# Moving the first units of the last MLP into attention steps 21 to 31, with their gating and modulation on ACT

## What is computed

```python
g1, b1, g2, b2, a1, a2 = jnp.split(cond, 6, axis=-1)          # per sequence, 128 numbers each
h = _layernorm(x) * g1[:, None, :] + b1[:, None, :]
q, k, v = ...                                                 # 16 heads of 8
attn = softmax(q k^T / sqrt(8));  o = attn v
o = o @ W_o.T + b_o
x = res1 + o * a1[:, None, :]                                 # gate the projection, add the residual
res2 = x
h = _layernorm(x) * g2[:, None, :] + b2[:, None, :]           # normalize, modulate
h = _gelu_tanh(h @ W_f1.T + b_f1) @ W_f2.T + b_f2
x = res2 + h * a2[:, None, :]
```

## Time and profile before

| | us |
|---|---|
| runs | 315.18, 310.84, 314.17 (median 314.17) |
| the profiled execution, its own time | 311.09 |
| its span | 309.2 |
| mean granted TensorE clock | 0.989 |
| PE busy | 277.3 (90%) |
| DVE busy | 241.7 (78%) |
| ACT busy | 188.9 (61%) |
| POOL busy | 175.6 (57%) |

### The profile page before, as it was taken

One profiled execution on the slowest core, in us unless ns is written; L12 is line 12 of the kernel. 1 busy time (PEld: TensorE's weight loads), 2 busy tenths in 40 slices (PEclk: granted clock), 3 DMA queues, 4 the chain that ended last, 5 costly groups with the idle time before them and its releaser, 6 DMA issues.

```text
span 309.2 us, 8237 instructions
## 1 busy us (share of the span) xinstructions
PE 277.3 (90%) x2900; PEld 154.6 (50%) x2900; DVE 241.7 (78%) x643; ACT 188.9 (61%) x355; POOL 175.6 (57%) x357
## 2 busy tenths in 40 slices
PE   2889999899889588799999999989868999999995
PEld 2444454454444345456656565656444445544444
DVE  5569999698899977688988888898955776776443
ACT  4457888788778547687778777776536222333330
POOL 8031765995996559677878696953345444223400
PEclk9999999999999989999999999999979999999999
DMA  7950000430340003425353444530000011011112
GB/s 240 329 117 2 2 0 4 112 102 2 94 119 2 0 7 85 123 71 155 88 152 102 128 121 106 149 77 8 4 4 4 0 34 34 2 34 35 35 36 68
DMA packets 26233, 21.58 MB, mean 70 GB/s; under 512 B 4400, under 2 KB 25552, under 8 KB 25936
## 3 DMA queue, kind: packets, MB, share of 16 engines
q1 hardware_dynamic: 25760, 20.37, 24.7%
q10 hardware_dynamic: 432, 0.67, 0.7%
HBM read 4.26 MB, written 2.10 MB: 21 GB/s over the span
## 4 chain that ended last, share of the span: by engine, by line
PE 55%; POOL 18%; DVE 14%; issue 9%; ACT 2%; DMA 1%; DVEq 0%; POOLq 0%; ACTq 0%
PE psum L280 47%; DVE mx L927 5%; POOL xn_tile L1121 2%; POOL q_rest L1066 2%; POOL q_part L1068 2%; DVE hid L874 2%; POOL q_part L1072 1%; POOL k_rest L1076 1%; PE psum L474 1%; PE psum L555 1%; DVE o_turn L934 1%; POOL rstd L1118 1%; PE psum L466 1%; PE psum L646 1%; PE psum L526 1%
## 5 line engine op out<-in xcount | busy, mean ns | idle before, releaser
L927 DVE TENSOR_REDUCE mx<-psum 128x8 f32<-128x1024 f32 x64 | 75.4, 1192 | 12.2 <-PE psum L280 11.8
L767 ACT ACTIVATE probs<-psum 128x1024 f32<-128x1024 f32 x64 | 65.5, 1023 | 11.8 <-PE psum L280 10.6
L280 PE MATMUL psum<-w_early,h0T 128*128 128x512 f32 x128 | 68.7, 622 | 0.0
L803 ACT ACTIVATE g_act<-psum,w_late 128x512 f32<-128x512 f32 x32 | 22.0, 688 | 44.7 <-PE psum L280 44.7
L280 PE MATMUL psum<-probs,v_pad 128*32 128x128 f32 x1024 | 41.7, 281 | 2.3 <-DVE o_turn L934 2.0
L280 PE MATMUL psum<-h2T,w_late 128*128 128x512 f32 x64 | 31.4, 607 | 0.0
L874 DVE SCALAR_TENSOR_TENSOR hid<-psum,rstd,gate 128x512 f32<-128x512 f32 x32 | 23.8, 743 | 8.2 <-PE psum L280 3.7
L280 PEld LDWEIGHTS psum<-probs,v_pad 128*32 128x32 f32 x1024 | 24.6, 109 | 10.4 <-ACT probs L767 3.8
L733 ACT ACTIVATE gate<-psum,rstd 128x512 f32<-128x512 f32 x32 | 22.0, 687 | 11.4 <-PE psum L280 6.8
L280 PE MATMUL psum<-g_act,w_late 128*128 128x512 f32 (+1 forms) x72 | 28.8, 545 | 0.0
L280 PE MATMUL psum<-k_st,q_st 64*128 64x128 bf16 x512 | 25.5, 220 | 1.9 <-DVE mx L927 1.9
(11 more groups left out here) (129 smaller groups left out, 551.5 us busy)
## 6 DMA issues: line engine op xcount, KB each, us to landing
q_st<-q_part SPq DMA_DIRECT2D x48, 128.0 KB
k_st<-k_part SPq DMA_DIRECT2D x48, 128.0 KB, 2.4
x_tok<-x SPq DMA_DIRECT2D x8, 256.0 KB, 7.4
out<-out_t SPq DMA_DIRECT2D x7, 256.0 KB, 2.3
w_late<-late SPq DMA_DIRECT2D x1, 1159.5 KB, 9.0
w_early<-early ACTq DMA_DIRECT2D x2, 256.0 KB, 5.3
k_st<-k_st SPq DMA_DIRECT2D x4, 128.0 KB, 5.0
q_st<-q_st SPq DMA_DIRECT2D x4, 128.0 KB
```

Source lines behind the costliest of these rows:

```text
L280: return nc.tensor.matmul(o, w, m, start=start, stop=stop, skip_group_check=shares)
L767: nc.scalar.activation(probs[:, n % 3, :, :, :].rearrange("p f j q -> p (f j q)"), psum[:, pair[0]:pair[1] + 1, :].rearrange("p a b -> p ( ...
L803: nc.scalar.activation(g_act[:, f, :], bank(2 + f % 2), ACT.Gelu_apprx_tanh, bias=wl("b_f1")[:, f:f + 1]).then_inc(c_gelu[f], 1)
L927: v.tensor_reduce(mx[:, c % 2, :, r, :], psum[:, pair[0]:pair[1] + 1, :].rearrange("p f (j k) -> p f j k", j=4), X_AXIS, ALU.max, negate=T ...
```

## The change

Nine units of the front stand in attention steps now, one in a step: proj 0 in step 21, res 0 in 23, proj 1 in 24, norm 0 in 25, res 1 in 27, proj 2 in 28, norm 1 in 29, res 2 in 30 and proj 3 in 31. Three of them (norm 1, res 2, proj 3) stood in `mlp(2)` and `mlp(3)` before. They all use bank 7 and take their turn in `SHARED_FILLS`; score fills keep all three pairs to the end. ACT gates the projections of groups 0 to 3, as scale times product plus a ready bias `b_gated` (one new DVE instruction in stage A), and modulates groups 0 and 1; the groups after these stay with DVE. `h2T` has two buffers. POOL's `layer_norm(0)` stands in step 24, `layer_norm(1)` in 28 and `layer_norm(2)` in 32.

```diff
--- before.py
+++ after.py
...
-FRONT = {27: ("proj", 0), 28: ("res", 0), 29: ("proj", 1), 30: ("norm", 0)}
-FRONT_END = {30: ("res", 1), 31: ("proj", 2)}
-FRONT_BANK = {("proj", 0): 5, ("res", 0): 6, ("proj", 1): 5, ("norm", 0): 6, ("res", 1): 5, ("proj", 2): 7}
-TWO_PAIRS = 27
+FRONT = {21: ("proj", 0), 23: ("res", 0), 24: ("proj", 1), 25: ("norm", 0), 27: ("res", 1), 28: ("proj", 2),
+         29: ("norm", 1), 30: ("res", 2), 31: ("proj", 3)}
...
-        if step >= TWO_PAIRS:
-            owner.append(0 if kind == "exp" else 1)
-        else:
-            owner.append(n % 2 if n < 2 * LEAD else n % 3)
+        owner.append(n % 2 if n < 2 * LEAD else n % 3)
...
+        if b in FRONT:
+            shared.append(FRONT[b])
...
-SHARED = {f: n for n, f in enumerate(SHARED_FILLS)}
+SHARED = {f: n for n, f in enumerate(f for f in SHARED_FILLS if f[0] != "res")}
...
-        h2T = sb("h2T", [D, GT])
+        h2T = sb("h2T", [D, 2, GT])
...
-                pe.wait_ge(shared_set, SHARED[fill] + 1)
+                if fill[0] == "res":
+                    pe.wait_ge(c_x2, fill[1] + 1)
+                else:
+                    pe.wait_ge(shared_set, SHARED[fill] + 1)
...
-                if g:
-                    pe.wait_ge(c_proj, g)
-                mm(bank(n), wl("wo"), tile_cols(feat, GRP * g, GRP)).then_inc(c_proj_mm, 1)
+                if g > 4:
+                    pe.wait_ge(c_proj, g - 4)
+                return mm(bank(n), wl("wo"), tile_cols(feat, GRP * g, GRP))
...
-                pe.wait_ge(c_proj, g + 1)
+                pe.wait_ge(shared_set, SHARED["proj", g] + 1) if g < 4 else pe.wait_ge(c_proj, g - 3)
...
-                n = FRONT_BANK[kind, g]
-                if (kind, g) == ("proj", 0):
-                    was, c, r = THIRD_PAIR_LAST
-                    pe.wait_ge(b_max if was == "max" else b_exp, 2 * c + r + 1)
-                if (kind, g) == ("norm", 0):
-                    pe.wait_ge(c_x2, 1)
-                if n == MISC_BANK:
-                    taken_out(SHARED_FILLS[-1])
+                shared_free(kind, g)
...
-                    output_projection(g, n)
+                    output_projection(g, MISC_BANK).then_inc(shared_mm, 1)
...
-                    residual(g, n)
+                    residual(g, MISC_BANK)
...
-                    normalized_features(g, n)
+                    normalized_features(g, MISC_BANK).then_inc(shared_mm, 1)
...
-                if b in FRONT_END:
-                    front(*FRONT_END[b])
...
-                if 2 < i < NG:
-                    output_projection(i, 7)
+                if 3 < i < NG:
+                    if i == 4:
+                        taken_out(SHARED_FILLS[-1])
+                    output_projection(i, 7).then_inc(c_proj_mm, 1)
...
+            def gate_projection(g):
+                act.wait_ge(shared_mm, SHARED["proj", g] + 1)
+                if g == 0:
+                    act.wait_ge(b_gated_set, 1)
+                if g:
+                    act.wait_ge(c_res_mm, g)
+                for s in range(GRP):
+                    b = GRP * g + s
+                    last = nc.scalar.activation(projT[:, s, :], bank(MISC_BANK)[:, s * P:(s + 1) * P], ACT.Identity,
+                                                bias=b_gated[:, b:b + 1], scale=mods[:, 4, b:b + 1])
+                last.then_inc(shared_set, 1)
+
+            def modulate(g):
+                act.wait_ge(shared_mm, SHARED["norm", g] + 1)
+                for s in range(GRP):
+                    b = GRP * g + s
+                    last = nc.scalar.activation(h2T[:, g % 2, s * P:(s + 1) * P], bank(MISC_BANK)[:, s * P:(s + 1) * P], ACT.Identity,
+                                                bias=mods[:, 3, b:b + 1], scale=mods[:, 2, b:b + 1])
+                last.then_inc(shared_set, 1)
+
...
+                kind, group = FRONT.get(b, (None, None))
+                if kind == "proj":
+                    gate_projection(group)
+                if kind == "norm":
+                    modulate(group)
...
+                    dve.wait_ge(bias_set, 2)
+                    v.tensor_tensor(b_gated[:, :], mods[:, 4, :], b_ov[:, :].to_broadcast([P, B]), ALU.mult).then_inc(b_gated_set, 1)
...
-                if b == 27:
-                    gate_projection(0, FRONT_BANK["proj", 0])
-                if b == 28:
-                    add_residual(0, FRONT_BANK["res", 0])
+                kind, group = FRONT.get(b, (None, None))
+                if kind == "res":
+                    add_residual(group, MISC_BANK)
...
-                if b == 31:
-                    statistics(1)
-                if b == 32:
-                    gate_projection(2, FRONT_BANK["proj", 2])
...
-                if b == 28:
-                    statistics(0)
-                if b == 29:
-                    gate_projection(1, FRONT_BANK["proj", 1])
-                if b == 30:
-                    modulate(0, FRONT_BANK["norm", 0])
-                    add_residual(1, FRONT_BANK["res", 1])
+                if kind == "res":
+                    statistics(group)
...
-                if b == 29:
-                    layer_norm(0)
-                if b == 32:
-                    layer_norm(1)
+                if b < B and FRONT.get(b - 1, (None, 0))[0] == "res" and FRONT[b - 1][1] < 2:
+                    layer_norm(FRONT[b - 1][1])
+                if b == B:
+                    layer_norm(2)
...
-            for g in range(2, NG):
+            for g in range(3, NG):
```

50 lines of the change are left out of this document (26 added, 24 removed).

## The result

The changed kernel takes 314.36 us (median of 22 runs, 311.6 to 318.0). The kernel before, run beside it, took 311.43 (22 runs, 309.12 to 315.52). The ratio is **1.0071 [1.0043, 1.0099]**: slower by a little, within the 2% that count as the same.

A forecast was written before the change was run, and what follows sets the result against it. PE, DVE or a chain through ACT was taken to bound each attention step, PE's order the last stage. 311.09 + 4.3 (steps) - 1.95 (last stage) + 0.2 (`b_gated`) = 313.6; 2.5 added to the middle, 312.6, gave 315.1 us, range 310.0 to 319.5.

The forecast's parts named there:

- step 30: Attention step with res 2, without maxima: from 6.8 us to 2.6, with no POOL wait and no low clock left.
- norm steps: Steps 25 and 29: PE waits for `xn` from POOL about 1.1 and 1.5 us; steps of 5.1 and 5.2 us.
- last stage: MLP stage: `mlp(2)` falls from 5.15 to 4.06 us, `mlp(3)` loses its output projection of 0.86; together -1.95 us.
- gating chain: Steps 21, 24, 28: late weighing, score block, projection, ACT's four gating instructions, exponential, next weighing; 4.53 us, taken as 4.5.
- Rival 3: ACT's gating and modulating instructions don't overlap, 0.46 us start to start instead of 0.35: +2.6 us, 317.7; chance 0.08.
- Rival 1: Slack hides ACT's gating, and POOL is early enough for the norms: -5.8 us against the sum, 309.3; chance 0.2.
- res steps: Steps 23 and 27, with PE's transposes and DVE's residual and statistics added: 4.05 us each.
- no stretch at half clock around step 30: Sign expected in the trace after the change: PE's clock does not fall to half near step 30.
- rival 2: Waits in steps 25 and 29 to 31 halve PE's clock: some 1.5 us per stretch, 316.6 to 318.1; chance 0.22.
- Rival 4: The last stage gives nothing back, as ACT's gelu or the features for `mlp(3)` set its pace: +1.95, 317.0; chance 0.05.
- `b_gated`: One new DVE instruction of 128x32 with a wait for its own engine: +0.2 us, between nothing and 0.4.
- third pair of banks: Score banks in steps 27 to 31: costs nothing and lets PE run further ahead.

The follow-up runs named there:

- e5: The changed kernel with DVE instead of ACT doing all gating and modulating at the new places; 313.77 us, ratio to the kernel before 1.0044.
- e10: The changed kernel with layer_norm ahead of scale_output on POOL, projections right behind the late weighing, and DVE gating in step 31; 310.22 us, ratio to before 0.9950.
- e11: The changed kernel with layer_norm ahead of scale_output on POOL and DVE gating in step 31; 310.46 us, ratio to the kernel before 0.9963.
- e1: The changed kernel with one 128x512 ACT gating instruction instead of four of 128x128 (values partly wrong); 313.45 us, ratio to the kernel before 1.0059.
- e2: The changed kernel with POOL's layer_norm of groups 0 and 1 leaving out the scaling (not normalized); 311.26 us, ratio to the kernel before 0.9976.
- e7: The changed kernel with layer_norm of groups 0 and 1 ahead of scale_output on POOL; 311.40 us, ratio to the kernel before 0.9994.
- e8: The changed kernel with two pairs of banks instead of three from step 27 on; 317.06 us, ratio to the kernel before 1.0183.

## Why the prediction was right, and where its terms were off

The forecast was 315.1, the measurement 314.36, inside 310.0 to 319.5; "within 2%" had 0.85. The sign and the size of the difference came out too: +2.5 predicted, +2.9 between medians, +3.2 ± 0.4 at equal clock, though +4.2 between the two profiled executions, for which the sum was made. The time itself had an error of its own: I set the kernel before at 312.6, the middle of four times, and its median beside the changed kernel was 311.43. With that base my sum would have said 313.9, 0.4 too low instead of 0.7 too high. In part the sum was lucky: step 30 was 1.2 us too short in it, the norm steps 0.3 too long and the last stage's gain 0.3 too small.

- **The gating chain** (4.53 predicted): 4.54, 4.54 and 4.55. ACT's four instructions took 1.39 us to the next exponential, with 1.40 predicted. Rival 3 (no overlap) is out. The estimate of 1.6 us worked out from the Trainium skill's "ScalarE: Activation LUTs", What ACT_TABLE_LOAD costs, was 0.2 us too long. The rule of that page of the Trainium skill (Rules for kernel authors) that additions and multiplications belong on VectorE held only where DVE had room: step 31 falls by 1.06 us with DVE (e5, e10, e11), step 28, where DVE was full, rises by 0.96 (e5).
- **Rival 1** (slack takes it up) fails at the place where I said it would be decided: PE waits for the exponential behind each gating, and e1 shows that shorter gating shortens those steps.
- **The norm steps** (5.1, 5.2): 4.99 and 4.98. The waits for `xn` were 0.89 and 1.20, not 1.1 and 1.5. I had called them the least sure terms; e2 and e7 show that they and what hangs on them are 2 us. What I didn't see is that they came from an order on POOL that costs nothing to change: I wrote that `layer_norm` "starts behind `scale_output`" and took it as given.
- **The res steps** (4.05): 3.97 and 3.96, as argued.
- **Step 30** (2.6, called the largest gain) took 3.78, since PE ran at half clock there, behind the waits of step 29; my sign "no stretch at half clock around step 30" didn't appear. This is rival 2 at one of its places: 3.78 against the 2.68 of e1, e2, e7, e10 and e11, which have no such stretch there, +1.1 us for my 1.5. That the prediction's forecast and this part of rival 2 were exclusive was wrong; both happened. In the median it is less than that, since not every execution has the stretch: four of the 22 had a mean clock of 1.000.
- **The last stage** (-1.95): -2.29. The iteration `mlp(2)` was mis-sized: 3.72 instead of 4.06, because I took it from `mlp(9)` as one without transposes. But `mlp(9)` has four of its own, of `yT`, at 301.15, 0.44 us ahead of its second layer, and `mlp(2)` has none. The rest of the gain, 2.29 - 1.43, is 0.86, exactly the predicted output projection of `mlp(3)`. Rival 4 is out.
- **`b_gated`** (+0.2): the first score block starts 0.30 us later. Not tested apart.
- **The third pair of banks** (no cost): it costs nothing and is worth about 1 us (e8). The sum needed no term for it, because my chains of steps 27 to 31 had no wait for a bank in them, which is what three pairs give.
